# Softmax reciprocals kept in spare columns of a PSUM score bank and taken at fixed places of VectorE's order

## The reference

```
q = layernorm(x) @ W_q;  k = ctx @ W_k;  v = ctx @ W_v        # 8 heads of 64
attn = softmax(mask(q k^T / 8))                               # over 750 keys, per head and query
x = x + tanh(g_xattn) * (attn v @ W_o + b_o)
h = gelu(bitlinear(layernorm(x), w1, b1))                     # 512 -> 2048
x = x + tanh(g_ffn) * bitlinear(h, w2, b2)                    # 2048 -> 512
# bitlinear: rmsnorm, then activations to 8 bits and weights to three values, then the product
```

## Time and profile before

| what | value |
|---|---|
| time, median of 3 runs | 1072.77 us (1072.48 to 1073.2) |
| the profiled execution's own time | 1070.9 us |
| its span, first to last instruction | 1069.1 us |
| mean granted TensorE clock | 0.990 of full speed |
| PE busy | 995.9 us, 93% |
| DVE / ACT / POOL busy | 835.2 / 805.7 / 712.1 us (78 / 75 / 67%) |

### The profile page before, as it was taken

How to read it: one execution, slowest core, us unless ns; L and a number is a source line. 1 busy time by engine, 2 the same in 40 slices (tenths; PEclk the granted TensorE clock), 3 DMA queues, 4 the chain that set the end, 5 groups by cost and what they waited for, 6 DMA issues and landing times. The chain is left out here.

```text
span 1069.1 us, 26540 instructions
## 1 busy us (share of the span) xinstructions
PE 995.9 (93%) x9856; PEld 579.5 (54%) x9856; DVE 835.2 (78%) x1707; ACT 805.7 (75%) x1374; POOL 712.1 (67%) x691
## 2 busy tenths in 40 slices
PE   3988899999999999999999998999999999999877
PEld 2455565565555655555556555556565565555443
...
GB/s 225 280 163 228 206 170 174 133 184 128 163 142 180 174 116 192 115 167 162 157 129 126 200 163 130 183 143 139 177 128 158 175 162 171 167 110 139 148 96 30
DMA packets 472335, 169.17 MB, mean 158 GB/s; under 512 B 450320, under 2 KB 452368, under 8 KB 471824
## 3 DMA queue, kind: packets, MB, share of 16 engines
...
...
## 5 line engine op out<-in xcount | busy, mean ns | idle before, releaser
L1339 POOL TENSOR_TENSOR p<-prob,p 128x750 f16<-128x750 f32 x224 | 358.5, 1614 | 110.4 <-ACT p L1189 108.1
L1007 DVE CUSTOM_DVE_ANT_0 prob<-ps_s,mbias 128x750 f32<-128x750 f32 x224 | 204.0, 933 | 58.8 <-PE ps_s L820 47.1
L1182 ACT ACTIVATE prob<-prob,rmin 128x750 f32<-128x750 f32 x224 | 204.3, 914 | 26.2 <-DVE rmin L1007 25.8
L787 PE MATMUL ps_g<-ctx,wk 128*128 128x375 f16 x1152 | 201.8, 327 | 23.4 <-POOL ctx L1350 16.4
L787 PE MATMUL ps_g<-wv,ctx 128*128 128x512 f16 (+1 forms) x864 | 197.0, 379 | 4.1 <-DVE k_sb L1026 2.2
L787 PEld LDWEIGHTS ps_g<-ctx,wk 128*128 128x128 f16 x1152 | 111.2, 99 | 105.6 <-issue 25.7
L820 PE MATMUL ps_s<-k_sb,q_sb 64*32 64x375 f16 (+2 forms) x2688 | 128.8, 322 | 15.6 <-DVE rmin L1007 15.4
L787 PEld LDWEIGHTS ps_g<-wv,ctx 128*128 128x128 f16 (+1 forms) x864 | 86.8, 103 | 101.0 <-issue 5.9
L849 PE MATMUL ps_g<-pt,v_sb 128*64 128x224 f16 (+2 forms) x2448 | 122.8, 254 | 2.6 <-DMA pt<-p 2.4
L1189 ACT ACTIVATE p<-prob 128x750 f16<-128x750 f32 x144 | 116.0, 820 | 3.5 <-DMA pt<-p 3.0
L849 PEld LDWEIGHTS ps_g<-pt,v_sb 128*64 128x64 f16 x2448 | 109.6, 110 | 2.9 <-issue 2.8
...
## 6 DMA issues: line engine op xcount, KB each, us to landing
...
```

The lines of the kernel that those rows point to most:

```text
L787: mm = nc.tensor.matmul(out, lhs, rhs, start=(m == 0), stop=(m == len(steps) - 1))
L1007: nc.vector.tensor_tensor_reduce(prob[:, (b * NU + n) % PROBS, :].rearrange("p (c k) -> p c k", c=2), ps_s[:, n % 2, :, 0:CH], mbias[:, :] ...
L1182: nc.scalar.activation(prob[:, (b * NU + n) % PROBS, :], prob[:, (b * NU + n) % PROBS, :], ACT.Exp, bias=rmin[:, n:n + 1], scale=-1.0, acc ...
L1339: nc.gpsimd.tensor_tensor(p16[:, u % HILO, 1, 0:J], prob[:, (b * NU + n) % PROBS, :], p16[:, u % HILO, 0, 0:J], ALU.subtract).then_inc(s[" ...
```

## The change

`rrec` is no tensor in SBUF any more, but 14 columns (384 to 397) of the first PSUM bank of the odd units' scores, which the scores leave unused. VectorE may touch that bank only while PE isn't writing it, so the reciprocals lose their own items: the new `recips_at` names for each odd unit the reciprocals that are taken directly ahead of its minimum `M`, after the wait for the scores and before PE is let go on to the next tile. For batches 0 to 14, groups 0 and 1 go ahead of units 7 and 11 of their own batch, groups 2 and 3 ahead of units 1 and 3 of the next batch. In the last batch, groups 0 to 4 go ahead of units 5, 7, 9, 11 and 13, and groups 5 and 6 stay items of DVE's list. All five lists are written anew; the items in them are the same, but for 65 of the 67 `R`.

```diff
+def recips_at(b, n):
+    if b == LB and n >= 5:
+        return [(b, (n - 5) // 2)]
+    return {1: [(b - 1, 2)] if b > 0 else [], 3: [(b - 1, 3)] if b > 0 else [], 7: [(b, 0)], 11: [(b, 1)]}.get(n, [])
...
-        rrec = sb("rrec", [128, NU], F32)
+        rrec = ps_s[:, 1, 0, 384:384 + NU]
...
                 if kind == "M":
 
                     need(dve, "scores", b, n // 2)
+                    if n % 2 == 1:
+                        for of in recips_at(b, n):
+                            take_reciprocals(*of)
                     need(dve, "mask_bias", b, 0)
                     need(dve, "p_lo", b, n - PROBS)
                     nc.vector.tensor_tensor_reduce(
...
 SP_SEQ = in_order("""
-    PD:0:0 LC:0:0 LX:0:0 LC:1:0 LC:2:0 PD:1:0 LM:0:0 XT:0:0 XT:1:0 WL:0:0 PD:2:0 LM:0:1 LC:0:1 WL:2:0 LX:0:1 WL:1:0
```

More of the change, by code:

```diff
@@ L84 @@
[L84 to L88, removed]
@@ new lines @@
+    F2:1:6 XQ:1:7 T:7:8 T:6:8 T:9:8 LR:1:8 T:8:8 HT:0:7 LR:0:9 LX:0:11 T:10:8 T:11:8 T:12:8 T:13:8 HT:1:7 F2:0:7
+    LM:0:10 T:0:9 XT:0:10 LC:2:10 XT:1:10 LR:1:9 LC:0:11 T:1:9 F2:1:7 T:3:9 T:4:9 T:2:9 LR:0:10 T:5:9 XQ:1:8 T:6:9
+    T:7:9 T:8:9 LC:1:11 T:9:9 T:10:9 T:11:9 T:12:9 T:13:9 LX:0:12 LM:0:11 LC:2:11 HT:1:8 T:0:10 XT:1:11 XT:0:11
+    T:2:10 T:1:10 XQ:0:9 T:4:10 LC:0:12 T:3:10 T:5:10 LC:1:12 T:6:10 T:7:10 XQ:1:9 T:8:10 T:9:10 F2:1:8 T:10:10
+    T:11:10 HT:0:9 T:12:10 LR:1:10 T:13:10 HT:1:9 F2:0:9 T:0:11 XT:0:12 XT:1:12 LC:2:12 F2:1:9 LM:0:12 T:2:11
@@ new lines @@
+    F1:7:3 V:4:5 K:4:5 PV:1:4 S:0:5 F2:0:3 V:5:5 S:1:5 K:5:5 K:6:5 K:7:5 Q:2:5 Q:3:5 S:2:5 PV:2:4 PV:3:4 S:3:5
+    F2:1:3 Q:0:6 S:4:5 Q:1:6 O:1:4 PV:0:5 S:5:5 V:0:6 V:1:6 V:2:6 K:0:6 S:6:5 K:1:6 V:3:6 K:2:6 V:4:6 PV:1:5 K:3:6
+    F1:4:4 F1:5:4 F1:6:4 F1:7:4 S:0:6 K:4:6 K:5:6 K:6:6 V:5:6 S:1:6 PV:2:5 Q:2:6 K:7:6 PV:3:5 S:2:6 Q:3:6 O:0:5
+    S:3:6 F2:1:4 O:1:5 Q:0:7 S:4:6 Q:1:7 V:0:7 F1:0:5 F1:1:5 F1:2:5 F1:3:5 K:0:7 S:5:6 K:1:7 PV:0:6 S:6:6 K:2:7
+    V:1:7 K:3:7 K:4:7 V:2:7 V:3:7 PV:1:6 S:0:7 F1:4:5 F1:5:5 F1:6:5 F1:7:5 V:4:7 Q:2:7 S:1:7 V:5:7 F2:0:5 K:5:7
@@ new lines @@
+    S:3:9 PV:3:8 F2:1:7 Q:0:10 S:4:9 Q:1:10 V:0:10 O:1:8 K:0:10 K:1:10 S:5:9 PV:0:9 K:2:10 K:3:10 V:1:10 K:4:10
+    S:6:9 F1:4:8 V:2:10 V:3:10 F1:5:8 F1:6:8 F1:7:8 K:5:10 S:0:10 PV:1:9 V:4:10 V:5:10 K:6:10 Q:2:10 S:1:10 K:7:10
+    PV:2:9 S:2:10 PV:3:9 Q:3:10 S:3:10 O:0:9 O:1:9 F2:1:8 S:4:10 Q:0:11 V:0:11 Q:1:11 S:5:10 F1:0:9 F1:1:9 F1:2:9
+    F1:3:9 V:1:11 PV:0:10 S:6:10 K:0:11 K:1:11 V:2:11 V:3:11 K:2:11 K:3:11 K:4:11 PV:1:10 S:0:11 F1:4:9 F1:5:9
+    F1:6:9 F1:7:9 K:5:11 S:1:11 V:4:11 K:6:11 K:7:11 V:5:11 F2:0:9 S:2:11 PV:2:10 PV:3:10 Q:2:11 Q:3:11 F2:1:9
@@ L151 @@
+    S:1:15 PV:2:14 PV:3:14 S:2:15 V:4:15 V:5:15 S:3:15 F2:0:13 S:4:15 O:0:14 O:1:14 PV:0:15 PV:1:15 F2:1:13 F1:0:14
+    F1:1:14 F1:2:14 F1:3:14 TX:1:14 S:5:15 PV:2:15 S:6:15 F1:4:14 PV:3:15 PV:4:15 F1:5:14 F1:6:14 F1:7:14 O:0:15
+    PV:5:15 F2:0:14 PV:6:15 PV:7:15 O:1:15 TI:2:14 TI:3:14 TX:0:15 TH:2:14 TH:3:14 F1:0:15 F1:1:15 F1:2:15 TX:1:15
+    F1:3:15 F1:4:15 F1:5:15 F1:6:15 F1:7:15 F2:1:14 TH:0:15 TI:0:15 TH:1:15 TI:1:15 F2:0:15 TH:2:15 TH:3:15 TI:2:15
     TI:3:15 F2:1:15 F3:1:15
@@ new lines @@
+    VL:4:14 KL:5:14 VL:5:14 G2:1:12 KL:6:14 M:4:14 M:5:14 XN:0:15 QL:3:14 PA:2:13 M:6:14 KL:7:14 PA:3:13 M:7:14
+    F2:1:12 XH:0:15 O:0:13 M:8:14 XH:1:15 L2:0:13 O:1:13 L3:0:13 KL:0:15 M:9:14 L2:1:13 KL:1:15 VL:0:15 VL:1:15
+    L3:1:13 M:10:14 F1:0:13 PA:0:14 KL:2:15 M:11:14 F1:1:13 F1:2:13 F1:3:13 KL:3:15 M:12:14 M:13:14 VL:2:15 QL:0:15
+    QL:1:15 GM:0:13 G2:0:13 M:0:15 KL:4:15 VL:3:15 PA:1:14 KL:5:15 M:1:15 F1:4:13 F1:5:13 F1:6:13 F1:7:13 QL:2:15
+    QL:3:15 M:2:15 M:3:15 KL:6:15 KL:7:15 GM:1:13 M:4:15 M:5:15 PA:2:14 PA:3:14 M:6:15 M:7:15 G2:1:13 VL:4:15
@@ L327 @@
+    PL:0:14 L:9:14 MB:0:15 H:10:14 XB:0:14 L:10:14 G2:0:13 L:11:14 H:12:14 PL:1:14 L:12:14 L:13:14 L:0:15 L3:0:13
+    L:1:15 H:2:15 L:2:15 G2:1:13 PL:2:14 PL:3:14 L:3:15 L:4:15 XB:1:14 H:5:15 L:5:15 L2:0:14 H:7:15 L2:1:14 L3:1:13
+    PL:0:15 L:6:15 L:7:15 PL:1:15 L:8:15 XB:0:15 L:9:15 L3:0:14 G2:0:14 PL:2:15 H:10:15 L:10:15 PL:3:15 L:11:15
+    H:12:15 L:12:15 L:13:15 PL:4:15 XB:1:15 L2:0:15 L3:1:14 PL:5:15 G2:1:14 PL:6:15 L3:0:15 PL:7:15 L2:1:15 L3:1:15
+    G2:0:15 G2:1:15
 """)
```

435 lines of the change are left out of this document (204 added, 231 removed).

## The result

The changed kernel takes 1042.04 us (median of 4 runs, 1040.62 to 1043.64); the kernel before, run beside it, 1072.62 (1072.18 to 1073.2). The ratio is 0.9715, with a 95% interval of 0.9698 to 0.9732: 30.6 us less. The forecast was 15.8 less, and the lower end of its range was 1046. So the two spans lie only 27.3 us apart.

The account below looks back on a forecast made before the run. PE, busy 93% of the span, was taken to bound the kernel. The terms, -22.0 - 1.7 + 1.8 - 0.9 - 2.0 + 2.0 + 7.0 = -15.8 us, took 1070.9 to 1055.1; 1.9 for the median gave 1057, range 1046 to 1071.

Parts of the forecast that it names:

- Terms 1 and 2: DVE's reciprocals no longer stall behind POOL: PE regains idle time (-22.0 us) and clock lost behind one gap (-1.7 us).
- Term 3: Reciprocals between even and odd minimum delay PE at two places with little cover, +0.5 and +1.3: +1.8 us.
- (d): New lists move XH, GM and DVE's KL among PE's items, so remaining stalls strike elsewhere: +7 us.
- term 1: PE's idle time behind reciprocals stalled by POOL on shared SBUF ports, summed over 17 gaps: -22.0 us.
- tight places: Places in PE's list with at most one PV or V between score tiles: 19 before, 7 after.
- (b): Batch 1: Q and O now stand between S:3 and S:4, removing the wait at 110.14 us: -2.0 us.
- (c): First batch: PV:0 no longer covers the minima of S:4: +2.0 us.
- (a): Start: POOL splits the second context chunk in its idle time before the variance, so PE starts sooner: -0.9 us.
- Rival 4: PE waits less in the new lists than in the old without stalls: 1042 to 1050 us, chance 0.14.
- Rival 1: New order gives the gain back as DVE's freed time goes into other waits: 1065 to 1072 us, chance 0.18.
- Rival 2: R in the pair delays the odd minimum 0.5 us 63 times, making it slower: 1075 to 1086 us, chance 0.09.
- Rival 3: Stall stays, because any small DVE instruction beside POOL suffers it: 1080.7 us, chance 0.03.

Follow-up runs that it names:

- e4: Kernel before, lists and places unchanged, both reciprocal parts made by reciprocal instructions of one SBUF input, taking away the stall alone (values differ): 1043.53 us, ratio 0.9744.
- e1: Lists of the kernel before (without the 65 R), with the reciprocals in PSUM and inside the pairs of minima: 1052.71 us, ratio 0.9816.
- e6: Changed kernel with the subtraction of line 1054 given a second operation (add 0.0) and a sum output, values the same: 1034.27 us, ratio 0.9650.
- e5: Changed kernel with PV:0:0 moved back between S:4:0 and S:5:0 in PE's order of the first batch: 1043.74 us, ratio 0.9731.
- e9: Changed kernel with a chain of three small dependent reciprocals ahead of line 952 in each of the 67 groups: 1053.81 us, ratio 0.9819.
- e3: Lists of the kernel before, reciprocals moved into the pairs of minima but rrec kept in SBUF, so the stall stays: 1090.02 us, ratio 1.0159.

## Why the prediction was wrong

**Terms 1 and 2, the stall (-23.7 foretold, -28.8 in e4).** Right in kind, 5.1 us short. Gap by gap I had reckoned 22.0 us of PE's idle time; PE's waits for DVE fell by 22.3, an agreement of the sum in which single places missed both ways. The clock was undersized: one stretch at 0.81 was counted for 1.7 us, and the mean granted clock gave back about 3.4; a further 3.3 us of PE's busy time that nothing in the prediction covers went too.

**Term 3, the pair (+1.8 foretold).** Its two places stand in the changed kernel's trace: `S:4` of the first batch waits 2.54 us where e4 has 2.00, and `S:6` of the last 1.51 (at 983.09), where +0.5 and +1.3 were foretold. A third wait of 0.84 us (`S:4` of batch 6, also with an `R` in its pair) was not counted. In the old lists the same way of counting gives 6.8 us against 6.7 more of waits for minima and 9.2 us of time. No run has the new lists without the pair, so what the pair costs there in time stays open.

**The new lists and (d), the step that failed.** The sum put +7 us on waits made anew ("a third of term 1"). Its ground was that about half of the 43.1 us had no stalled reciprocal ahead; but those waits are the 21 us that term 1 leaves standing anyway (20.8 in e4), so they speak for nothing new, and no row gave the 7 its size. With the stall gone, pair and lists together were foretold 1.8 + 6.1 = +7.9 us and measured 1042.0 - 1043.5 = -1.5 (the changed kernel against e4; by the ratios -3.1, with some 4 us either way). The steps in between are +9.2 for the pair in the old lists and -10.7 for the lists. Idle time in the steady part fell from 16.9 in e1 to 4.9 us, PE's waits for row minima from 18 to 5, and those for `rrec` from 4 (3.1 us) to none, while head and tail stayed (28.1 and 14.5 us against 28.5 and 14.7). PE's waits for DVE came to 18.4 us, below e4's 20.8, so nothing was made anew on balance. I had read the old lists' 19 tight places against the new ones' 7, and used them only for the price of the reciprocals; that with fewer tight places waits would go too got no term. What (d) described did happen at one place: a stalled subtraction struck elsewhere, at 149 to 152 us, and its relief with all else gave 9.3 us (e6). It was line 1054, though, which the prediction does not name, and not `XH` (line 1058). In the sum: -28.8 + 9.2 - 10.7 = -30.3 (the steps share their ends, so this has to come near the -30.6 measured and proves nothing more). Of the 14.8 us that the forecast missed by, 5.1 are the stall and 9.4 pair and lists, (d) above all.

**(b)**, -2.0 foretold, was not won: the wait ahead of `S:4` of batch 1 went, and `O:1` in front of it waits the same 2.00 us for POOL's `attn`. **(c)** stood in the trace and cost nothing (e5). **(a)** came to -1.8 instead of -0.9. POOL's idle 0.97 us was filled as foretold, and besides its power took 0.84 us in place of 2.51, which nothing in the prediction covers, while the first chunk began 0.49 us later and the first two together took 4.01 us in place of 3.2. POOL's timeline of the changed kernel:

```profile
12.11 0.84 POOL L1373 TENSOR_TENSOR rs<-ve,half_neg 112x2 f32<-112x2 f32 x1
```

**Rivals.** Rival 4 came true (1042 to 1050, chance 0.14): (d) is nothing or a small gain. The result stands at the rival's very edge because the stall gave 5 us more than its term. Rival 1 (given back) did not happen. Rival 2 did not either, by its own sign: the waits for row minima are 8.8 us, not above 15. Its mechanism is real where a pair grows by another half microsecond, at a third of the full price in the new orders (e9), and with the stall left in it decided the sign in the old ones (e3, 1090). Rival 3 is out: no case above 0.19 us in three lines of 67.

**What should have shown it.** Lines 952 and 955 at 0.16 (foretold 0.15 to 0.2), PE busy 993.8 (994), DVE busy 788.6 (783) and both 2 us waits of the first batch were met. Off were PE's idle time, 48.0 for 59, its waits for DVE, 18.4 for 30, and the first product, 14.66 for 15.5. The page of the Trainium skill that was weighed against the choice for PSUM ("Perfetto Trace Analysis", section "Optimizing Scalar/DVE Operations", 60 and 125 ns of access) is not seen: 161 ns with a PSUM operand against at best 169 and 160 without.

What stays open: the 3.3 us of PE's busy time in e4; what the pair costs in the new lists, and so what these are worth without it; which of the moved items matter; and whether an order written for e6's kernel would win more, as `XH` has a case of 5.50 us there.
